# A decoder kernel on one core: norms applied by VectorE, a re-ordered issue of scores, feed-forward and tail

## The reference, cut to what matters

```
LN(x) = (x - mean) * (var + eps)^-0.5, eps = 1e-5; softmaxes are over all keys
x = LN(x + attn0(x))               16 heads of 64, projected from 256
x = LN(x + cross0(x, ctx))         16 heads of 16, keys and values from the 120 context rows
x = LN(x + ffn0(x))                quantized SiLU gate: 256 -> 1024 -> 256
x = LN(x + block(x)), with block:  h = LN(x) g + b; a = causal gated attention of h
                                   y = x + a; y + W2 (leaky ReLU(W1 (LN(y) g + b)))^2
x = LN(x + cross1(x, ctx, ctx)):   scores of two key sets, softmax over the queries;
                                   z0 = LN(q + weighted values) g0 + beta0
                                   z1 = LN(z0 + relu(z0 Wo + bo)) g1 + beta1
x = LN(x + coupled(x)):            3 times: x = x + coupling(x) * twist(x), where coupling is a
                                   GELU network 256 -> 256 -> 128 -> 64 -> 1 per token and one
                                   of the mean over the tokens
```

## Time and profile before

| what | us |
|---|---|
| median of 3 runs | 1455.36 |
| lowest, highest | 1446.14, 1455.41 |
| the profiled execution: its time | 1455.32 |
| its span, first to last instruction | 1453.6 |
| mean granted TensorE clock | 0.932 |
| busy: PE, DVE, ACT, POOL | 1190.9, 734.6, 742.5, 380.2 |

### The profile page before, as it was taken

The page is one execution under the profiler, slowest core; times in us unless marked ns, Lnnn a source line. Parts: engine busy times, 40 slices in busy tenths (PEclk is TensorE's granted clock), DMA queues, the critical chain, the costliest instruction groups (busy, mean ns, idle before and its releaser), DMA issues.

```text
span 1453.6 us, 18465 instructions
## 1 busy us (share of the span) xinstructions
PE 1190.9 (82%) x6450; PEld 801.0 (55%) x6458; DVE 734.6 (51%) x1791; ACT 742.5 (51%) x1890; POOL 380.2 (26%) x881
## 2 busy tenths in 40 slices
PE   6876887899778897799977888788978888779956
PEld 3454644577455554477655564457745555457644
DVE  0266166457445435755535525655743544855643
ACT  1354344548446533656635634464844653555833
POOL 1133200054204420034302431005420442005420
PEclk9999998999988999999988999899989899989977
DMA  9200300000000000000000000000000000000000
GB/s 248 77 8 1 123 10 1 1 1 1 15 0 23 1 15 0 1 0 1 16 1 1 23 1 15 1 1 1 1 1 1 16 1 0 1 1 1 1 1 14
DMA packets 29991, 22.69 MB, mean 16 GB/s; under 512 B 14476, under 2 KB 29260, under 8 KB 29772
## 3 DMA queue, kind: packets, MB, share of 16 engines
q1 hardware_dynamic: 29308, 19.93, 5.2%
q10 hardware_dynamic: 592, 1.59, 0.3%
HBM read 19.42 MB, written 2.10 MB: 15 GB/s over the span
## 4 chain that ended last, share of the span: by engine, by line
PE 58%; DVE 17%; ACT 9%; POOL 9%; issue 6%; DMA 1%; SPq 0%; ACTq 0%; POOLq 0%; DVEq 0%
PE PS L519 8%; PE PS L918 7%; POOL work L2032 7%; PE PS L506 7%; PE PS L659 4%; PE PS L688 3%; PE PS L567 3%; PE PS L894 3%; PE PS L783 2%; PE PS L580 2%; DVE stat L1552 2%; PE PS L930 2%; ACT x_room L1219 2%; PE PS L494 2%; PE PS L767 1%
## 5 line engine op out<-in xcount | busy, mean ns | idle before, releaser
L2018 POOL TENSOR_TENSOR rstd<-var,minus_half 128x2 f32<-128x2 f32 x80 | 56.4, 705 | 568.9 <-DVE nmean L1562 568.9
L2013 POOL TENSOR_TENSOR pool_pause<-minus_half 128x1 f32<-128x1 f32 x96 | 18.7, 195 | 447.6 <-DVE inv L1634 366.5
L1219 ACT ACTIVATE x_room<-res,nshift,rstd 128x256 f32<-128x256 f32 x128 | 69.7, 593 | 127.7 <-POOL nshift L2020 127.6
L1466 ACT ACTIVATE work<-PS,nmax 120x256 f32<-120x256 f32 x256 | 118.6, 483 | 24.2 <-DVE nmax L1892 23.3
L918 PE MATMUL PS<-x_room,work 128*120 128x256 f32 x512 | 119.8, 384 | 3.7 <-ACT x_room L1211 3.7
L1267 ACT ACTIVATE work<-PS,nmax 128x256 f32<-128x256 f32 x256 | 118.1, 480 | 5.8 <-DVE nmax L1627 5.8
L2032 POOL TENSOR_SCALAR work<-work,inv 128x256 f32<-128x256 f32 x256 | 118.2, 483 | 0.0
L1627 DVE TENSOR_REDUCE nmax<-PS 128x2 f32<-128x512 f32 x128 | 82.2, 684 | 61.4 <-PE PS L645 60.7
L1892 DVE TENSOR_REDUCE nmax<-PS 120x2 f32<-120x512 f32 x128 | 86.3, 686 | 53.2 <-PE PS L918 52.7
L659 PE MATMUL PS<-ident,work 128*128 128x128 f32 x512 | 74.9, 293 | 46.7 <-POOL work L2032 46.4
L2072 POOL TENSOR_SCALAR work<-work,head_mask 128x120 f32<-128x120 f32 x256 | 107.7, 448 | 0.0
(11 more groups left out here) (267 smaller groups left out, 2529.7 us busy)
## 6 DMA issues: line engine op xcount, KB each, us to landing
x_room<-in_x_dram SPq DMA_DIRECT2D x4, 512.0 KB, 4.3
xa<-in_x_dram SPq DMA_DIRECT2D x4, 512.0 KB, 3.9
out_dram<-x_room SPq DMA_DIRECT2D x4, 512.0 KB, 3.5
rows<-in_rows_dram ACTq DMA_DIRECT2D x1, 1536.0 KB, 8.7
late<-in_L_attn_W_dram SPq DMA_DIRECT2D x2, 768.0 KB, 7.4
wv<-in_L_attn_kernel_dram SPq DMA_DIRECT2D x2, 512.0 KB, 9.4
wq<-in_L_attn_kernel_dram SPq DMA_DIRECT2D x2, 512.0 KB, 9.4
wk<-in_L_attn_kernel_dram SPq DMA_DIRECT2D x2, 512.0 KB, 7.8
```

The source lines that it names most:

```text
L1219: op = act.activation(dst[:, t, :], src(t), ACT.Identity, scale=rstd[:, t:t + 1], bias=nshift[:, t:t + 1])
L1466: op = act.activation(e1[:, par, r, kv, :], bank(SCORE_1[n % 4])[0:M, kv * S:(kv + 1) * S], ACT.Exp, bias=nmax1[:, par, r, kv:kv + 1], acc ...
```

## The change

- Norms are applied on DVE: `apply_norm` is now one `tensor_scalar` a tile with two operands in memory, (x - mean) * rstd; `nmean`, `nshift` and POOL's second instruction are gone.
- Norms "3" and "h" share one statistic: DVE makes two variances, POOL one power for both; POOL writes norm "3", DVE writes "h" from `res`.
- `attn0` on DVE: `max0(u+1)`, `inverse0(u)`, `keep_e0t(u-1)`.
- `cross0`: PE issues scores two steps ahead of the transposes, ACT exponentials one ahead of the copies; DVE's order at the end is its own.
- `ffn0`: `down(t)` now stands ahead of `up(t+1)` or of the next fill; four of eight `queries0` are left for later stages (two in `attn1`, two at the head of `cross1`).
- `cross1`: products of 32 rows. `k1m` holds two copies (even and odd heads of a row group), two steps are issued as a pair on neighbouring row groups, `scores_1(n)` waits for one exponential more. `turn_back(0)`, the turn of z0(0), its `keep` and `out_1(0)` stand inside the loop.
- Tail: the chain for b = 0 runs ahead of that for b = 1; z1's gain is multiplied in while it is centred, and norm z1 is never written out (`centre_z1`, `sum_5`). All `keep_k0` are on ACT.
- Coupling network: the fill stands behind the cycle's last product; `max0(then, 0)` stands behind all cycles on DVE.

```diff
-    for u in range(U0 + 2):  (DVE, attn0)
-        if 1 <= u <= U0:
-            inverse0(it, u - 1)
         if u + 1 < U0:
             max0(it, u + 1)
+        if u < U0:
+            inverse0(it, u)
+        if 1 <= u <= U0:
+            keep_e0t(it, u - 1)
...
+            def apply_norm(it, name, src, dst, b):   (DVE)
+                dve.wait_ge(rstd_ready[name].sem, rstd_ready[name].at(it, b + 1))
+                for t in range(TS * b, TS * b + TS):
+                    op = dve.tensor_scalar(dst[:, t, :], src(t), mv[:, t, 0:1], rstd[:, t:t + 1], ALU.subtract, ALU.mult)
+                op.then_inc(normed[name].sem, 1)
...
-                    mm = pe.matmul(bank(SCORE_1[n % 4])[0:M, kv * S:(kv + 1) * S], k1m[:, g % 2, kv, 2 * r + par, :],
-                                   q1[:, c, b * S:(b + 1) * S], start=True, stop=True)
+                    for r in (n % HP, n % HP + 1):
+                        rows = slice(32 * r, 32 * (r + 1))
+                        mm = pe.matmul(bank(SCORE_1[r])[0:M, kv * S:(kv + 1) * S], k1m[g % 2][rows, kv, par, :],
+                                       q1[rows, c, b * S:(b + 1) * S], start=True, stop=True)
...
+                for n in range(UX):   (PE, cross0)
+                    if n + 2 < UX:
+                        scores_x(it, n + 2)
+                    turn_x(it, n)
+                    if then is not None and n % 2 == 0:
+                        values0(then, 2 + n // 2)
+                    if n % 2 == 0 and n > 0:
+                        weigh_x(it, n // 2 - 1, then)
+                out_x(it, 0)
+                weigh_x(it, NB * KD - 1)
+                if then is not None:
+                    values0(then, 6)
+                out_x(it, 1)
+                if then is not None:
+                    values0(then, 7)
...
+                gate(it, 2)           (PE, ffn0)
+                turn_hidden(it, 0)
+                down(it, 0)
+                up(it, 2)
+                context1(it, 1)
+                gate(it, 3)
+                turn_hidden(it, 1)
+                down(it, 1)
+                up(it, 3)
+                if then is not None:
+                    queries0(then, 1)
+                turn_hidden(it, 2)
+                down(it, 2)
...
+                sum_z1(0)             (DVE, tail)
                 scale_values(2 * GX - 1)
+                norm_summed(it, "z1", 0)
                 keep_o1(GX - 1)
+                centre_z1(0)
                 stats_z0(1)
+                sum_5(0)
+                apply_norm(it, "z0", z0_of, xs["z0"], 1)
+                norm_summed(it, "5", 0)
+                apply_norm(it, "5", of(res), xs["5"], 0)
+                sign_5(0)
+                sum_z1(1)
+                norm_summed(it, "z1", 1)
+                centre_z1(1)
+                sum_5(1)
+                norm_summed(it, "5", 1)
+                apply_norm(it, "5", of(res), xs["5"], 1)
+                sign_5(1)
...
     (PE, coupling_net: keys0(then, J - 2 + r) or scores0(then, 0) moved from
      behind the second product to behind the fourth, the one of tf_done)
```

More of the change, by code:

```diff
@@ L263, in decoder @@
         q1 = view(x3_room, 0, P, [KD, N])
-        k1m = view(work, E, P, [2, 2, HC, M])
+        k1m = [view(x1_room, 544 * i, P, [2, 2, M]) for i in range(2)]
         HP = HC // 2
@@ L1213, in keep_queries @@
                 op.then_inc(signal_kept.sem, 1)
-            def apply_norm(it, name, src, dst, b):
-                act.wait_ge(shift_ready[name].sem, shift_ready[name].at(it, b + 1))
-                for t in range(TS * b, TS * b + TS):
-                    op = act.activation(dst[:, t, :], src(t), ACT.Identity, scale=rstd[:, t:t + 1], bias=nshift[:, t:t + 1])
-                op.then_inc(normed[name].sem, 1)
-            def of_res(t):
-                return res[:, t, :]
             def keep_cross_weights():
@@ L1295, in attn0 @@
                         keep_e0t(it, u - 1)
-                    if last is not None and u in (5, 6):
-                        apply_norm(last, "out", of_res, y, u - 5)
                     if u == 2 and first_pass(it):
@@ L1333, in ffn0 @@
-            def ffn0(it, then=None):
+                exp_x(0)
+                for n in range(UX):
+                    if n + 1 < UX:
+                        exp_x(n + 1)
+                    m = n // 2
+                    act.wait_ge(tx_done.sem, tx_done.at(it, n + 1))
+                    if m > 1:
+                        act.wait_ge(avx_done.sem, avx_done.at(it, m - 1))
+                    act.copy(ext[:, m % 2, :, n % 2 * P:(n % 2 + 1) * P],
+                             PS[0:M, 4:6, :].rearrange("p a (h s) -> p (a h) s", s=P)).then_inc(tx_kept.sem, 1)
+                    if then is not None and n % 2 == 0:
+                        keep_v0(then, 2 + n // 2)
@@ L1542, in _ @@
             one_pass(NI - 1, last=NI - 2)
-            for b in range(NB):
-                apply_norm(NI - 1, "out", of_res, y, b)
         @blk.vector
@@ L1815, in attn1 @@
                 op.then_inc(lf_ready.sem, 1)
-                for hf in range(TS):
-                    dve.wait_ge(om_done.sem, om_done.at(it, hf + 1))
-                    dve.tensor_tensor(pair(om, hf), tokens_of(TOKEN_X[hf]), broad(row["L1_attn_bo"]), ALU.add).then_inc(om_biased.sem, 1)
+                keep_vm(1)
+                bias_om(1)
                 dve.wait_ge(fcol_done.sem, fcol_done.at(it, 1))
@@ L1859, in attn1, with cross1 @@
                     norm_summed(it, "4", b)
-            def cross1(it, then=None):
+                    apply_norm(it, "4", of(res), xs["4"], b)
+            def cross1(it):
                 def scale_values(m):
@@ L1994, in one_pass @@
                 attn1(it)
-                cross1(it, then)
+                cross1(it)
                 coupled_ffn(it, then)
-            keep_first()
             max0(0, 0)
```

569 lines of the change are left out of this document (286 added, 283 removed).

## The result

| | before | after |
|---|---|---|
| median, four runs of each (us) | 1454.51 | 1395.47 |
| lowest, highest | 1446.14, 1455.41 | 1380.85, 1401.50 |
| ratio, 95% interval | | 0.959 (0.951 to 0.967) |
| span of the profiled execution | 1453.6 | 1387.8 |
| mean granted TensorE clock | 0.932 | 0.900 |

What follows compares the result with a forecast made beforehand. No engine bounds the kernel throughout; PE comes nearest, itself binding only cross1's score loop, with chains through DVE, POOL and ACT elsewhere. Terms sum to -140 us on 1455.3, plus 25 allowed: 1340, range 1300 to 1400.

Steps and rivals of the forecast that it cites:

- attn0: First attention stage: DVE's reciprocal ahead of its copy removes PE's wait for POOL, 34 us gained, bounds 14 and 38.
- allowance of 25: Whole run: 25 us added to the forecast time for small waits that a followed schedule misses.
- rival C: Norms: DVE's in-order queue becomes the bound, its 0.8 us waits for POOL add 51 us, giving 1391; chance 0.14.
- score loop: cross1: 32-row pairs at 1.06 us make ACT the bound, loop 37.0 against 39.8 us, 11 gained in all.
- the mechanism among the rivals: attn0: PE's clock stays at 1.2 GHz after waits, making the kernel slower than before, up to 1538 us; chance 0.03.
- Rival D: cross1's score loop: 32-row products don't run side by side, 42.4 us a loop, 1362 in all; chance 0.05.
- cross0: First cross stage: new order and freed norm 2 give 14.0 us a filled pass, 6 the last, 48 in all.
- ffn0: Feed-forward stage: up behind down makes DVE wait before its third and fourth tiles, 16.5 us lost in all.
- attn1, MLP and head of cross1: Earlier norm h and fills covering PE's waits: gains of 7 us for attn1 and MLP, 6 for cross1's head.
- Tail: Last exponential to last c0 turn: 19.2 us instead of 27.3, 31 gained in all, bounds 18 to 36.
- Coupling: Coupling network: moving the key fill into PE's wait shortens its cycles, 20 us gained in all, bounds 8 to 27.
- it would be wrong if: Failure signs: DVE's waits for POOL in the chain, pairs taking 1.8 us, or PE's clock below 0.9 in attn0 or loop.

Runs made afterwards that it cites:

- e4: The changed kernel with 64-row score products in cross1, two steps side by side, four masked key copies per group in place of two: 1346.78 us, 0.931.
- e8: The kernel before with only DVE's order in attn0 changed (maxima of u+1, reciprocal of u, copy of u-1): 1406.46 us, 0.969.
- e12: The kernel before with the new order of cross0, and norm 2 alone applied by DVE in place of ACT: 1413.71 us, 0.979.
- e9: The kernel before with the new order of cross0 alone, norms still on ACT: 1438.05 us, 0.995.
- e10: The 64-row version with ffn0's third and fourth up products moved earlier, the fourth ahead of both first down products: 1323.03 us, 0.915.
- e11: The 1333.0 us version (64 rows, up products first), with DVE applying norm m's first half after the third tile's four small operations: 1333.09 us, 0.9225.

## Why the forecast was right and where it was wrong

The range held with some luck. The loop lost 44.7 us where 11 were to be gained, attn0 gave 11 more than forecast, and the allowance of 25 took up part of the rest. That the time lies near rival C's 1391 is chance too: its mechanism cost nothing that the runs show.

**The step that failed** is the score loop. "I take 1.06 for a pair" held nearly (1.13). "ACT's eight exponentials ... need 3.6 and become the bound" made PE the engine with pauses in a stage where it had stood at full clock by being busy for 39.28 of 39.8 us, and I priced that stage at 2.4 GHz all the same. I had the mechanism among the rivals, but put it in attn0, where PE was to become busier, and gave it 0.03. The place to look for it was where the change takes work from PE. The loop cost 44.7 us instead of giving 11. Even at full clock the 37.0 was too low: e4's loop of 41.2 (39.3 counted as in the forecast) shows a cycle of 4.10, not 3.85, and insertions that come through with 4.7 instead of 4.4 (39.3 less eight cycles and the 1.8 at the start). Nor did ACT become the bound: it is busy for 34.6 us of e4's 41.2.

**Rival D** (pairs not side by side) was false: two 32-row pairs back to back take 1.15 us (x16 above), two of 64 rows 1.99. The Trainium skill (TensorEngine Tiling (Array Packing), Tiling Modes) would have had the engine drain at each change of tiling; between 32-row scores and column groups the trace shows no gap that a wait doesn't explain, so the sum was right to leave it out.

**attn0** was under-sized, 45.1 for 34: units stand 3.10 apart as forecast (783.89 from 780.79), but the first pass, taken like the others, gave 15.3 us, and the second 11.7. e8 confirms the cause.

**cross0**: 43.6 for 48. Two steps take 7.9 us (7.7 forecast); a filled pass gives 14.6 to 14.8 (14.0). The 6 us of the last pass did not come: without fills it went from 45.4 to 46.1, at a clock of 0.93 for 1.00. Of the 14, the forecast's 7 for norm 2 measured 4.4 to 6.1 (e12), the order 4.1 to 6.0 (e9), the query fill 1.9.

**ffn0**, the term against the change, was right in size (17.2 for 16.5) and place; DVE's waits were 2.23 and 4.21, forecast 1.2 and 3.7. That it can be undone e10 shows.

**attn1, MLP and head of cross1** failed by 20 us. "A half norm so falls from 3.5 to about 2.8" held: norm m takes 2.82 us from its first statistic to the end of its application where it took 3.48 (the changed kernel, then the one before, third pass):

```profile
915.73 0.75 DVE L1547 BATCH_NORM_STATS2 stat<-res 128x6 f32<-128x256 f32 x2
...
917.81 0.74 DVE L1566 TENSOR_SCALAR x_room<-res,mv,rstd 128x256 f32<-128x256 f32 x2 [0.84 <-POOL rstd L2059]
```

```profile
984.71 0.75 DVE L1552 BATCH_NORM_STATS2 stat<-res 128x6 f32<-128x256 f32 x2
...
987.10 1.09 ACT L1219 ACTIVATE x_room<-res,nshift,rstd 128x256 f32<-128x256 f32 x2 [4.55 <-POOL nshift L2020]
```

But the second half now starts 1.5 us later (7.64 us after the stage's start, 6.14 before), since DVE first waits for POOL and applies the first half itself, and ends 0.8 later. That wait (0.8 each time, 41 us in the run) is rival C's mechanism; it was present and cost nothing in e11's place, as PE covers it. By the same token the shorter norms bring nothing: in the last pass, without fills, the two stages take 18.3 and 34.0 us before, 18.4 and 33.9 after. And the cover of the fills was over-counted. In attn1's head PE idles 2.33 us of the third pass with one fill (18.70 less 16.37) and 2.33 with two (20.20 less 17.87); I had taken this wait as gone. From the attention to the loop two fills brought PE's idle time from 2.93 to 1.44 us, and the stage is 1.3 us longer.

**Tail**: 20.1 us from the last exponential to the last c0 turn in the third pass, forecast 19.2, before 27.3. **Coupling**: -21.6 for -20; the third cycle's projections take 3.84 us instead of 5.41.

The forecast's "it would be wrong if ... PE's clock fell below 0.9 in attn0 or the loop" is what happened in the loop (attn0 stood at 0.94 to 0.99), and the allowance of 25, meant for small waits, was used up by attn1 and the tail.

## What to carry to other kernels

A change that makes PE's work in a loop shorter than the trip around it must be priced at both clocks: if the loop was at 1.00 with a PE that hardly paused, ask what will keep it there. Of two packings that fit the same round trip try the wider one first; here 64 rows held the clock, but for one short fall in each traced run, where 32 did not, at the same 1.13 us. And an instruction moved from one engine to another pays where its old engine's queue held it up (7.1 us for norm 2), not by the difference of two durations.

## What the runs showed that I had not expected

- A lone pair of 32-row products takes 1.13 us, the same as a pair of 64 rows; only two pairs of 32 rows in succession run together (16 instructions in 1.15 us, 1.99 with 64 rows).
- With equal cycles and equal waits, from 316 to 332 us in the first pass, the clock then stood at 1.00 for 64-row products and fell to 0.5 for 32-row ones; the same 32-row products issued three times over held it at 1.00. The Trainium skill (TensorE: Matmul & The Clock Gate, Why this matters for your kernels) advises to slice small contractions at 32 rows so that they run concurrently; the trace agrees that they do (16 instructions in 1.15 us, where 64 rows take 1.99) and shows what it can cost.
- Where the clock falls the kernel's time becomes uncertain: 20 us between runs, against 2 to 6 for the 64-row versions.
- POOL took 1.29 us for one 128x256 application of norm 3 where DVE takes 0.41 to 0.50.
